# Criss-cross attention: the residual through a ring of SBUF buffers and a GpSimd add, and another order of VectorE's score work

## The reference, cut to what matters

```
x: [8, 512, 96, 96]   Wq, Wk: [64, 512]   Wv: [512, 512]
q, k, v = 1x1 convolutions of x (with biases)
eH = einsum('bchw,bcpw->bhwp', q, k), -inf where p == h      # along a column
eW = einsum('bchw,bchp->bhwp', q, k)                         # along a row
att = softmax(concat([eH, eW], axis=3), axis=3)
outH = einsum('bcpw,bhwp->bchw', v, att[..., :96])
outW = einsum('bchp,bhwp->bchw', v, att[..., 96:])
return gamma * (outH + outW) + x
```

## Time and profile before

| | |
|---|---|
| median of 3 runs | 4620.48 us (4616.53 to 4622.32) |
| the profiled execution, its own time | 4611.6 us |
| its span, first to last instruction | 4609.9 us |
| mean granted TensorE clock | 0.846 |
| HBM read and written | 832.83 MB and 339.74 MB, 254 GB/s |
| seven batch elements with items | 550.7 to 558.8 us each |

### The profile page before, as it was taken

One profiled execution on the slowest core, in us unless ns is written; L12 is line 12 of the kernel. 1 busy time (PEld: TensorE's weight loads), 2 busy tenths in 40 slices (PEclk: granted clock), 3 DMA queues, 4 the chain that ended last, 5 costly groups with the idle time before them and its releaser, 6 DMA issues.

```text
span 4609.9 us, 96212 instructions
## 1 busy us (share of the span) xinstructions
PE 3574.8 (78%) x33624; PEld 2455.4 (53%) x33624; DVE 2519.6 (55%) x3802; ACT 1879.4 (41%) x3852; POOL 849.0 (18%) x1075
## 2 busy tenths in 40 slices
PE   3987888678787797877877788877889668884854
PEld 2544656446564565545655466543666446563744
DVE  6645665366553764537644476444665366553733
ACT  2535634165242652326532364314634156341610
POOL 0000231102311032110311014120131102311221
PEclk9998789878898698987988879888799888896666
DMA  7957699976999679995899968998599986999499
GB/s 284 293 187 245 184 278 285 308 242 184 300 272 316 217 194 311 266 312 190 214 312 279 299 192 230 300 287 285 178 270 289 300 255 187 282 280 280 96 277 274
DMA packets 824037, 1179.24 MB, mean 256 GB/s; under 512 B 56560, under 2 KB 574192, under 8 KB 823536
## 3 DMA queue, kind: packets, MB, share of 16 engines
q1 hardware_dynamic: 453840, 680.92, 47.5%
q10 hardware_dynamic: 314400, 340.86, 22.7%
q0 software_dynamic: 55296, 151.02, 17.0%
HBM read 832.83 MB, written 339.74 MB: 254 GB/s over the span
## 4 chain that ended last, share of the span: by engine, by line
issue 38%; PE 25%; DMA 13%; SPq 12%; DVE 4%; POOL 3%; ACT 3%; ACTq 1%; POOLq 0%; DVEq 0%
DMA v_in<-v_pixel_major 10%; SPq L369 9%; PE banks L1005 5%; PE banks L1006 5%; PE banks L1007 5%; PE banks L1079 3%; PE banks L1081 3%; PE banks L1080 3%; SPq L360 3%; DMA out<-acc 2%; POOL prob_col L461 1%; POOL qk_pair L443 1%; PE banks L1057 1%; ACT v_out L563 1%; DVE x_lo L776 1%
## 5 line engine op out<-in xcount | busy, mean ns | idle before, releaser
L1005 PE MATMUL banks<-wv_hi,x_hi 128*128 128x512 f16 x2304 | 940.4, 408 | 222.7 <-DVE x_lo L776 188.1
L784 DVE SCALAR_TENSOR_TENSOR v_out<-banks,proj,v_out 128x512 f16<-128x512 f32 x576 | 431.5, 749 | 1228.1 <-ACT v_out L563 1228.1
L1006 PE MATMUL banks<-wv_lo,x_hi 128*128 128x512 f16 x2304 | 934.1, 405 | 0.0
L1007 PE MATMUL banks<-wv_hi,x_lo 128*128 128x512 f16 x2304 | 928.6, 403 | 0.0
L1079 PE MATMUL banks<-prob_row,v_in 96*128 96x96 f16 x3072 | 488.2, 220 | 399.3 <-DMA v_in<-v_pixel_major 357.8
L563 ACT ACTIVATE v_out<-banks,proj 128x512 f16<-128x512 f32 x576 | 390.0, 682 | 949.6 <-PE banks L1007 940.3
L443 POOL TENSOR_TENSOR qk_pair<-qk_f,qk_pair 128x256 f16<-128x256 f32 x288 | 209.6, 728 | 2531.0 <-ACT qk_pair L579 2524.1
L867 DVE SCALAR_TENSOR_TENSOR acc<-banks,att,acc 128x384 f32<-128x384 f32 x768 | 443.9, 609 | 394.0 <-PE banks L1081 393.2
L1079 PEld LDWEIGHTS banks<-prob_row,v_in 96*128 96x128 f16 x3072 | 324.6, 106 | 447.7 <-issue 345.3
L1045 PE MATMUL banks<-k_hi,q_both 128*96 128x96 f16 x1536 | 363.5, 294 | 243.4 <-ACT prob_row L618 190.4
L469 POOL DMA_DIRECT2D acc<-x x384 | 346.9, 977 | 933.3 <-DVE acc L867 913.2
(11 more groups left out here) (104 smaller groups left out, 7171.6 us busy)
## 6 DMA issues: line engine op xcount, KB each, us to landing
v_in<-v_pixel_major SPq DMA_DIRECT2D x768, 384.0 KB, 7.7
x_raw<-x ACTq DMA_DIRECT2D x290, 512.0 KB, 8.2
x_next<-x SPq DMA_DIRECT2D x384, 384.0 KB, 3.8
v_pixel_major<-v_out ACTq DMA_DIRECT2D x576, 256.0 KB, 4.6
acc<-x POOLq DMA_DIRECT2D x384, 384.0 KB, 10.0
out<-acc SPq DMA_DIRECT2D x384, 384.0 KB, 15.1
qk_halves<-qk_pair ACTq DMA_DIRECT2D x288, 128.0 KB, 4.7
x_first<-x SPq DMA_DIRECT2D x24, 768.0 KB, 8.1
```

What stands on the lines that cost most here:

```text
L784: nc.vector.scalar_tensor_tensor(out=v_out[tile % V_OUT][:, :, 1, :], in0=bank[tile % 2][:, :].rearrange("p (t c) -> p t c", t=CT), scalar ...
L1005: nc.tensor.matmul(dst, s_hi, m_hi, start=(t == 0), stop=False)
L1006: nc.tensor.matmul(dst, s_hi, m_lo, start=False, stop=False)
L1007: last = nc.tensor.matmul(dst, s_lo, m_hi, start=False, stop=(t == CT - 1))
```

## The change

The residual is no longer added by the transfer. SP loads a chunk of `x` into one of three buffers `xr` of 128 x 768 float32 (`load_residual`), GpSimd waits for it and adds it to `acc` with a `tensor_tensor` (the semaphore `res_added` now counts GpSimd's adds), and SP stores the chunk. SP issues the first three loads of a half at the end of its column stage, and each further one directly behind the store of the chunk three before it. `STORE_LAG` becomes 6. The ring of v buffers is cut from 6 to 4. On VectorE, pair `p`'s maxima, scaling and shift come ahead of the pair's item, and the sum of pair `p - 1`'s even half comes behind it.

```diff
@@ -50,12 +50,15 @@
     HALF = 2 * NG * TT
     GROUPS = TP * HALF
 
-    VU = 6
+    VU = 4
+    XR = 3
     LOADS = GROUPS // TT
     assert LOADS % VU == 0 and CT % TT == 0
 
     CH = 2 * G * W
     NCH = HW // CH
+    CHUNKS = CT * NCH
+    assert CHUNKS % XR == 0
 
     SCW = 1536
     SCAN = HW * CT // SCW
@@ -73,7 +76,7 @@
     DEAL = (T_ITEMS - TURN) // 2
     assert T_ITEMS == 2 * DEAL + TURN
     RES_LAG = 2
-    STORE_LAG = 14
+    STORE_LAG = 6
     PROLOGUE_LAG = 4
     PROLOGUE_SCAN = 4 + 3 * (SCAN - 1) + PROLOGUE_LAG
     assert PROLOGUE_SCAN + 10 < ITEMS
@@ -147,6 +150,7 @@
     qk_f32, _ = place("qk_f32", [P, BLK], F32)
     qk_pair = [place(f"qk_pair{s}", [P, 2, BLK], F16)[0] for s in range(2)]
 
+    xr = [place(f"xr{u}", [P, CH], F32)[0] for u in range(XR)]
     v_in = [place(f"v_in{u}", [L, G, TT, 2, P], F16)[0] for u in range(VU)]
 
     nmax, factor = {}, {}
@@ -249,7 +253,8 @@
         col_act = sem("col_act")
         col_dve = sem("col_dve")
         row_added = sem("row_added")
-        res_added = [[sem(f"res_added{tt}_{c}") for c in range(NCH)] for tt in range(TT)]
+        xr_loaded = [sem(f"xr_loaded{u}") for u in range(XR)]
+        res_added = sem("res_added")
         out_stored = [[sem(f"out_stored{tt}_{c}") for c in range(NCH)] for tt in range(TT)]
 
 
@@ -287,6 +292,9 @@
 
         def row_number(g):
             return g // HALF * (HALF // 2) + g % HALF - HALF // 2
+
+        def chunk_number(g):
+            return g // HALF * (TT * NCH) + (g % HALF - HALF // 2) // (2 * TT) * TT + g % TT
 
         def col_number(g):
             return g // HALF * NG + g % HALF // TT
@@ -365,8 +373,15 @@
             def store_chunk(b, g):
                 tp, o, h, tt = group_at(g)
                 px = slice(h // 2 * CH, (h // 2 + 1) * CH)
-                sp.wait_ge(res_added[tt][h // 2], b * (TP * 16) + tp * 16 + 16)
+                sp.wait_ge(res_added, b * CHUNKS + chunk_number(g) + 1 + XR)
                 sp.dma_start(out_acc[b, tp * TT + tt, :, px], acc[tt][:, px]).then_inc(out_stored[tt][h // 2], 16)
+
+            def load_residual(b, n):
+                tp, c, tt = n // (TT * NCH), n // TT % NCH, n % TT
+                sp.wait_ge(res_added, b * CHUNKS + n + 1)
+                sp.dma_start(xr[n % XR][:, :], x_acc[b, tp * TT + tt, :, c * CH:(c + 1) * CH]).then_inc(
+                    xr_loaded[n % XR], 16
+                )
 
             def batch(b, items):
                 load_qk(b)
@@ -387,14 +402,23 @@
                     tp, o, h, tt = group_at(g)
                     if tt and g // TT + VU < LOADS:
                         load_v(b, g // TT + VU)
+                    if g % HALF == HALF // 2 - 1:
+                        for n in range(XR):
+                            load_residual(b, g // HALF * (TT * NCH) + n)
                     if g % HALF >= STORE_LAG:
                         tp, o, h, tt = group_at(g - STORE_LAG)
                         if o == ROW and h % 2:
                             store_chunk(b, g - STORE_LAG)
+                            n = chunk_number(g - STORE_LAG) + XR
+                            if n < (g // HALF + 1) * (TT * NCH):
+                                load_residual(b, n)
                     if g % HALF == HALF - 1:
                         for last in range(g - STORE_LAG + 1, g + 1):
                             if group_at(last)[2] % 2:
                                 store_chunk(b, last)
+                                n = chunk_number(last) + XR
+                                if n < (g // HALF + 1) * (TT * NCH):
+                                    load_residual(b, n)
 
             with sp.Fori(0, SCAN // FIRST) as i:
                 for k in range(FIRST):
@@ -414,6 +438,7 @@
         @block.gpsimd
         def _(pool):
             pool.sem_inc(qk_ready, QK_READY0)
+            pool.sem_inc(res_added, XR)
             nc.gpsimd.memset(ident[:, :], 0.0).then_inc(ident_zero, 1)
             nc.gpsimd.memset(diag_bf[:, :, :], 0.0).then_inc(ident_zero, 1)
             pool.wait_ge(ident_zero, 2)
@@ -466,9 +491,11 @@
                 tp, o, h, tt = group_at(g)
                 px = slice(h // 2 * CH, (h // 2 + 1) * CH)
                 pool.wait_ge(row_added, b * (GROUPS // 2) + row_number(g) + 1 + ONE0)
-                pool.dma_start(
-                    acc[tt][:, px], x_acc[b, tp * TT + tt, :, px], accum_op=ALU.add
-                ).then_inc(res_added[tt][h // 2], 16)
+                n = chunk_number(g)
+                pool.wait_ge(xr_loaded[n % XR], b * (CHUNKS // XR * 16) + (n // XR) * 16 + 16)
+                nc.gpsimd.tensor_tensor(acc[tt][:, px], acc[tt][:, px], xr[n % XR][:, :], ALU.add).then_inc(
+                    res_added, 1
+                )
 
             def batch(b, items):
                 LA = AHEAD + 2
@@ -821,8 +848,6 @@
                     nmax[o][:, both].rearrange("p (u g) -> p u g", u=2), pair_strips[p % 2], AX_X, ALU.max,
                     negate=True,
                 ).then_inc(nmax_raw, 1)
-                if p > 0:
-                    sum_even(b, p - 1)
                 dve.wait_ge(nmax_raw, n + 1)
                 nc.vector.tensor_scalar(
                     nmax[o][:, both], nmax[o][:, both], att[0:L, S_FACTOR:S_FACTOR + 1], None, ALU.mult
@@ -925,9 +950,11 @@
                     if items:
                         item(b + 1, k)
                 for p in range(PAIRS):
+                    score_pair(b, p)
                     if items and p < NP:
                         item(b + 1, HEAD + p)
-                    score_pair(b, p)
+                    if p > 0:
+                        sum_even(b, p - 1)
                     if items:
                         for c in scan_at_pair(p):
                             if c % 2 == 0:
```

## The result

The changed kernel takes 4437.6 us (median of 4 runs, 4430.9 to 4447.0) against 4621.4 for the kernel before, measured beside it: ratio 0.9605, 95% interval 0.9583 to 0.9628. That is 184 us faster, where 357 were predicted; the time lies inside the range. The profiled execution took 4432.2 us.

What follows compares the result with a forecast made beforehand. The DMA engines were taken to bound the row stages and what follows them. 4611.6 - 263 (296 less 33 for the rings) - 94 (scores) = 4255 us profiled, so 4264 us predicted, range 4114 to 4466.

Steps and rivals of the forecast that it cites:

- The DMA part: Row stages and what follows them: loading the residual's 151 MB plainly saves 33.5 engine-us per MB, 296 us in all.
- The scores: Pairs of scores: VectorE's new order saves 10 us per element in row pairs, 3 in column pairs, 94 us.
- The shorter rings: Row stage and turn: fewer v and residual buffers sometimes let the queue run low, share 1.05 for 1.07, costing 33 us.
- the other end is half of the gain: Worst case of the shorter rings: row stage and turn at a share of 0.99, taking 117.1 us.
- I cost both at nothing while landings stay under some 9 us: Work behind GpSimd's wait for residual loads, `low_qk` and row stage 1's products of line 461, costs nothing.
- GpSimd's adds: 24 adds of 1.64 us per row stage, 39.5 us; GpSimd busy 77 of 88 us, off the path, costing nothing.
- the 49 us kept for that: VectorE's line 776 slowed beside GpSimd's adds: at worst 3.5 us per row stage, 49 for 14; taken as 0.
- A, rings too short: Rival: the DMA share settles at 0.99 and the residual's gain halves to 155 us; 4371 us, chance 0.14.
- B: Rival: the scores gain nothing, the wait only moves from ScalarE's exponents to VectorE's low v part; 4358 us, chance 0.09.
- C: Rival: the residual's accumulation costs the DMA engines no time, so only the scores gain; 4527 us, chance 0.08.
- D: Rival: slower, the residual ring serialises SP at its wait ahead of the store, v loads behind it; 4686 us, chance 0.05.
- The sign for A and D: The DMA share of the row stages falling under 1.0 would show the forecast wrong.

Runs made afterwards that it cites:

- plain_overwrite: The kernel before with GpSimd's residual transfers writing plainly instead of accumulating, the sum with the attention left out; 4296.9 us, ratio 0.9308.
- v6_second: pool_order with six v buffers in place of four in the second half of every batch element; 4340.1 us, ratio 0.9399.
- before_vu4: The kernel before with four v buffers in place of six, residual still accumulated by transfers; 4670.8 us, ratio 1.0099.
- pool_order: The changed kernel with GpSimd's adds 8 groups behind instead of 2, own places in the turn, stores 10 instead of 6; 4389.7 us, ratio 0.9506.
- combo3: gp_loads and v6_second together, with three residual buffers in each half; 4243.9 us, ratio 0.9195.
- gp_loads: pool_order with residual loads issued by GpSimd on its own queue, each behind the add that frees its buffer, not by SP; 4290.4 us, ratio 0.9277.
- score_only: The kernel before with only VectorE's new order in the pairs of scores; 4527.0 us, ratio 0.9792.
- ring6_second: The changed kernel with six residual buffers instead of three in the second half of each batch element; 4486.6 us, ratio 0.9703.

## Why the prediction was right and wrong

**What bounds the kernel: right.** The row stages were bound by the DMA engines. Taking work off the engines gave 316 us, with nothing else changed but GpSimd's own time per issue, off its path (plain_overwrite).

**The DMA part: right for the accumulation, too high for the change as made.** plain_overwrite gains 316 us, with ends 278 and 322 said. But the changed kernel takes only 232 us of the engines' time away and not 316, which is 24.6 engine-us per MB in place of 33.5, and at the 1.07 of the prediction's sum 217 us and not 296. The term that was mis-sized is "so I take 49.5 per MB". The residual's own packets cost about that (q1's packets of 3072 bytes grew by 48 engine-us per MB). But the other transfers got dearer beside them, which the prediction puts at nothing: the v loads' packets rose from 59 to 63 ns on the mean, 80 us of each engine over the span, and q10 by 24. In plain_overwrite they stayed at 60. Why sharing SP's queue does this is open.

**The scores: right in sum.** 94 said, 95 measured. By itself the new order gives 10.2 us per element in the row pairs, where 10 was said, and 1.3 in the column pairs for 3; with the residual's part it is 13.7 and 1.6. The exponents' wait fell to 121.3 us, just over the "under 120" that stood there.

**The shorter rings: the larger miss.** The prediction says: "I take a share of 1.05 for 1.07, nearer the first end because 8.5 us of queued work is still much more than nothing", and prices it at 33 us. Of the 217 us just worked out, 84 came through, so the waits took 133; that is 100 us of the residual's miss, and the DMA part is the other 79. The fault is visible in its own numbers. Its sentence just before asks for landings under 8.7 us; 8.5 us of queued work is by itself 8.5 us until the last of these loads lands. The two leave no slack, and the landing came out at 8.8 and 9.6 us at the median of the two row stages of the second batch, 9.2 in the round shown. I read a full queue as a sign that the engines are fed, and it is also the delay of each load in it. A round of 11.57 us then sets a chunk per 3.86 us, and the ring, not the engines, paces the adds. Yet the adds are not the row stage: v6_second has the same ring and landings of 9.9 us, and its row stage 2 is down at 73.7 us. The late adds cost by what stands behind them in GpSimd's order, and the four v buffers cost by themselves; the term has one price for the two rings and none for the order.

Also in this term: "the other end is half of the gain" for the first stretch. Measured, less than that is left (84 of 316), because several losses come together, and four v buffers alone cost the kernel before 48 us (before_vu4).

**"I cost both at nothing while landings stay under some 9 us": failed with it.** The bound itself was wrong: in row stage 1 the median landing was 8.8 us, under it, and what stands behind GpSimd's wait was late all the same: `low_qk` (90.7 us of VectorE's waits) and the products (134.0 us of TensorE's). Letting them pass is worth 48 us (pool_order), and 42 even with loads in time.

**Together**, for the 232 us given back against plain_overwrite: the v ring 48 (before_vu4, both halves) or 50 (v6_second, second half alone), GpSimd's order 48 or 42, the loads in SP's queue 99 or 105, their dearer work included. That is 195 to 197 us. combo3, which has all three at once, is 194 us faster than the changed kernel. Each was measured in two settings (the v ring gives 50 us on pool_order and 46 on gp_loads), so they nearly add. Some 35 us stay open. An estimate from the other side agrees: plain_overwrite with the 95 us of the scores would take 4202 us, 42 less than combo3. The adds on GpSimd, their contention with VectorE, and the four v buffers of the first halves lie in there; they weren't separated.

**GpSimd's adds: a little low.** 1.64 us estimated, 1.86 measured. Line 803 (776 before) takes 1380 ns on the mean, for 1317 before, at the same median of 1274, so its 289 instructions take 18 us more over the span, inside the 49 us kept for that. In gp_loads, with GpSimd busier, the mean is 1466.

**The rivals.** A, rings too short, came nearest, and a part of it is the mechanism (the v ring, 48 to 50 us), with 4371 us in place of 4437.6: the share of the first stretch was to fall to 0.99 and fell to 0.94. Its time counts no work held up behind GpSimd, and no dearer v packets. B is refuted by score_only, C by plain_overwrite. D was at work as well: SP does stand at the store until the add is done, and the landing in row stage 2 (9.6 us) came near the 10.6 from which D makes the kernel slower. It did not get there. The time lies inside the range by luck: the high end, 4466 us, is A without any gain in the scores, and here the scores gained in full while the residual's part gained 71 us less than in A. My 0.62 for the forecast was too much, with a landing bound 1.3 us under the only landing of that stream that the trace showed.

**The signs.** "Wait for `v_in` well under 368" came true, and the row pairs fell below 56 us, to 51.4. q1 grew by 151 MB, but by 56 engine-us for each ((0.614 x 4430.4 - 0.475 x 4609.9) x 16 / 151), not about 50. "Row stage and turn about 110, at a share of 1.03 to 1.06" and "row stage 2 and the next head about 140" did not come: they are 123.9 us at 0.94, and 82.7 + 63.9 = 146.6 us. The sign for A and D, a share under 1.0 in the row stages, did not show there (1.02 and 1.07); it was the turn that fell to 0.76. So the signs as written would have cleared the ring.

What stays open is also how much of gp_loads' 99 us is the moment of issue, because there a load goes out behind the add, and in pool_order behind the store. ring6_second issued loads earlier in SP's queue and lost, which speaks for the queue; the issue moment alone, in a queue of its own, wasn't tried, nor were plain loads of 3072-byte packets from GpSimd's queue.

## What to carry to other kernels

An accumulating transfer can cost the DMA engines nearly twice what a plain one does (83.0 engine-us per MB for 43.2 here); the share of its queue shows it. What its replacement costs is read from all queues together, since transfers beside it can get dearer: here a quarter of the forecast saving was lost that way. Whoever replaces it by loads and an add on an engine must work out the ring's round (landing + add + issue, against the time per buffer that the stage allows), with the landing taken from the queued bytes ahead of the load, and must ask what stands behind the new wait in that engine's order: late adds by themselves cost little here. A stream with few buffers was better off in a queue of its own. Which ring to deepen has to be measured: in SP's queue three more residual buffers cost 49 us, and two more v buffers in the same halves won 50.

## What the runs showed of the hardware

- A plain load from GpSimd's queue goes in larger packets than an accumulating one: 30720 packets for the 151.02 MB that take 55296 before, and 43.2 engine-us per MB. The same loads added 55296 packets and 56 engine-us per MB to q1 when SP issued them.
- The DMA share stood at 1.00 to 1.09 in the row stages shown, whether they moved 271 or 357 GB/s; in the turn of plain_overwrite it was 1.06 at 402. In these rows the share tells that the engines are busy, and the GB/s tell what they achieve.
- Issuing a DMA took GpSimd 977 ns on the mean when it accumulates (before) and 552 when it doesn't (plain_overwrite); in gp_loads it was 0.56 us, 17 times in row stage 1. GpSimd, 18% busy over the span before, was busy 58.91 of 76.8 us there.
